# A Mamba block with a SwiGLU layer on one core: 32 products per batch, whose results nobody reads, are left out

## The reference

```
h  = x * rsqrt(mean(x*x) + 1e-5) * norm_w
xs, res = split(h @ in_proj_w.T)                      # 256 + 256 channels
u  = silu(causal conv of 4 taps over xs + conv_b)
delta, Bm, Cm = split(u @ x_proj_w.T)                 # 64 + 16 + 16
delta = softplus(delta @ dt_proj_w.T + dt_proj_b)
state[t] = exp(delta[t] * A) * state[t-1] + delta[t]*u[t]*Bm[t]   # 256 channels x 16 states
y  = (sum over states of state*Cm + u*D) * silu(res)
x1 = layernorm(x + (y @ out_proj_w.T + x))
out = layernorm(x1 + (silu(x1 @ wg.T) * (x1 @ wu.T)) @ wd.T)      # 384 hidden
```

## Time and profile before

| | us |
|---|---|
| median of 3 runs | 560.69 (560.64 to 561.02) |
| the profiled execution, its own time | 562.91 |
| its span, first to last instruction | 561.1 |
| PE busy | 522.8 |
| DVE busy | 495.8 |
| POOL busy | 414.2 |
| ACT busy | 385.8 |

### The profile page before, as it was taken

The page is one execution under the profiler, slowest core; times in us unless marked ns, Lnnn a source line. Parts: engine busy times, 40 slices in busy tenths (PEclk is TensorE's granted clock), DMA queues, the critical chain, the costliest instruction groups (busy, mean ns, idle before and its releaser), DMA issues.

```text
span 561.1 us, 7049 instructions
## 1 busy us (share of the span) xinstructions
PE 522.8 (93%) x2161; PEld 272.9 (49%) x2161; DVE 495.8 (88%) x559; ACT 385.8 (69%) x625; POOL 414.2 (74%) x212
## 2 busy tenths in 40 slices
PE   8989998999999999999999999999999997668695
PEld 6444444545564536545564536544564534433363
DVE  5867789998999999999999999999999999998863
ACT  3676896599478975699478974799478974554231
POOL 8769677996579874996589874996589874996310
PEclk9979999999999999999999999999999999759798
DMA  8062305600624032700624032600634042700000
GB/s 224 9 151 56 96 8 143 151 0 2 150 59 111 1 73 78 167 4 0 151 62 108 0 82 70 169 0 0 150 63 106 0 90 60 168 2 0 0 20 19
DMA packets 27391, 39.29 MB, mean 70 GB/s; under 512 B 3832, under 2 KB 10072, under 8 KB 27360
## 3 DMA queue, kind: packets, MB, share of 16 engines
q1 hardware_dynamic: 25168, 38.38, 28.7%
q10 hardware_dynamic: 2192, 0.55, 0.5%
HBM read 3.27 MB, written 2.10 MB: 10 GB/s over the span
## 4 chain that ended last, share of the span: by engine, by line
PE 74%; DVE 9%; issue 6%; ACT 5%; POOL 2%; DMA 1%; SPq 1%; POOLq 0%; DVEq 0%; ACTq 0%
PE dense_ps L508 18%; PE y_ps L500 9%; PE dense_ps L526 9%; PE dense_ps L577 7%; DVE state L1196 6%; PE dense_ps L584 3%; PE c_ps L484 3%; PE dense_ps L528 2%; PE dense_ps L533 2%; PE dense_ps L545 2%; PE y_ps L498 2%; PE dense_ps L547 2%; PE dense_ps L551 2%; PE dense_ps L549 2%; PE dense_ps L541 2%
## 5 line engine op out<-in xcount | busy, mean ns | idle before, releaser
L1018 POOL TENSOR_TENSOR prod<-du_rep,b_rep 128x2048 f32<-128x2048 f32 x63 | 286.0, 4544 | 71.9 <-ACT b_rep L778 50.0
L1196 DVE TENSOR_TENSOR_SCAN state<-decay_ps,prod 128x512 f32<-128x512 f32 x256 | 298.9, 1207 | 17.3 <-ACT decay_ps L731 10.6
L731 ACT ACTIVATE decay_ps<-delta_rep,a_neg 128x512 f32<-128x512 f32 x252 | 170.0, 689 | 71.8 <-DVE state L1196 71.6
L1206 DVE TENSOR_TENSOR state<-state,c_ps 128x1536 f32<-128x1536 f32 (+1 forms) x63 | 122.8, 1949 | 19.0 <-PE c_ps L484 14.8
L508 PE MATMUL dense_ps<-x_all,ident 128*128 128x256 f32 x476 | 121.8, 398 | 5.6 <-ACT z_pos L757 3.6
L508 PEld LDWEIGHTS dense_ps<-x_all,ident 128*128 128x128 f32 x476 | 88.5, 195 | 48.4 <-issue 15.6
L500 PE MATMUL y_ps<-state,gather 128*32 128x512 f32 x504 | 70.8, 635 | 4.6 <-DVE state L1206 4.6
L526 PE MATMUL dense_ps<-h_t,tap_t 128*128 128x512 f32 x128 | 58.4, 598 | 0.9 <-ACT h_t L789 0.9
L1040 POOL TENSOR_TENSOR state<-state,c_rep 128x512 f32<-128x512 f32 x40 | 51.4, 1285 | 4.3 <-ACT c_rep L774 4.2
L484 PE MATMUL c_ps<-bc,pick 64*128 64x512 f32 x64 | 31.6, 493 | 8.4 <-DVE state L1206 8.4
L526 PEld LDWEIGHTS dense_ps<-h_t,tap_t 128*128 128x128 f32 x128 | 23.2, 189 | 30.5 <-issue 29.4
(11 more groups left out here) (201 smaller groups left out, 691.3 us busy)
## 6 DMA issues: line engine op xcount, KB each, us to landing
du_rep<-z_wm SPq DMA_DIRECT2D x64, 256.0 KB, 5.0
delta_rep<-z_ln SPq DMA_DIRECT2D x64, 256.0 KB, 4.5
out_dram<-y_out SPq DMA_DIRECT2D x7, 256.0 KB, 4.7
state<-L_attn_in_proj_w_in ACTq DMA_DIRECT2D x1, 256.0 KB, 3.9
x_all<-L_attn_x_in SPq DMA_DIRECT2D x1, 256.0 KB, 4.2
state<-L_ffn_w_gate_in SPq DMA_DIRECT2D x1, 192.0 KB, 10.0
state<-L_ffn_w_up_in SPq DMA_DIRECT2D x1, 192.0 KB, 3.5
state<-L_ffn_w_down_in SPq DMA_DIRECT2D x1, 192.0 KB, 4.3
```

The lines of the kernel that those rows point to most:

```text
L731: A(decay_ps[n % DECAYS][:, :], decay_ps[n % DECAYS][:, :] if spread_first else delta_rep[:, h, c, :], ACT.Exp, scale=a_neg[:, col:col + 1 ...
L1018: TT(prod[quad % 2][:, :, :], du_rep[:, h, :, :], b, ALU.mult).then_inc(prod_ready, 1)
L1196: dve.tensor_tensor_scan(state[n // BLOCKS % 2][:, n % BLOCKS, :], decay_ps[n % DECAYS][:, :], prod[n // BLOCKS % 2][:, n % BLOCKS, :], 0. ...
L1206: TT(state[quad % 2][:, mine, :], state[quad % 2][:, mine, :], c_ps[:, :].unsqueeze(1).broadcast_to([P, BLOCKS - mine.start, T]), ALU.mult ...
```

## The change

All 32 "F" entries are taken out of `PLAN`. The real jobs keep their order. `stir` itself, the idle products of head and tail, all tables of the other engines and all waits of the real jobs stay as they were.

```diff
-        PLAN = [["Fh", "Fh", "Fh", "Fh", "Fh", "Fh", "Fh", "Fh", "C", "Fh", "S", "h"],
+        PLAN = [["C", "S", "h"],
                 ["proj", "xs0", "C", "S", "xs1"],
-                ["res0", "res1", "C", "Fxd", "Fxd", "Fxd", "Fxd", "Fxd", "S"],
-                ["xd", "Fz0", "Fz0", "S", "x1", "Fz0", "Fz0", "z0", "C"],
-                ["z1", "Fgate0", "Fgate0", "Fgate0", "Fgate0", "Fgate0", "S", "Fgate0", "Fgate1", "Fgate1", "Fgate0", "Fgate0", "Fgate1", "gate0", "C", "gate1", "d0"],
+                ["res0", "res1", "C", "S"],
+                ["xd", "S", "x1", "z0", "C"],
+                ["z1", "S", "gate0", "C", "gate1", "d0"],
                 ["S", "gate2", "C", "d1", "b0"],
-                ["up0", "up1", "up2", "S", "Fb1", "b1", "C", "down", "Fb2", "Fb2"],
+                ["up0", "up1", "up2", "S", "b1", "C", "down"],
                 ["b2", "b3", "C", "S"]]
```

## The result

The changed kernel takes 572.17 us (median of 4 runs, 571.72 to 572.79). The kernel before, run beside it, takes 560.86 us. The ratio is 1.0206, with a 95% interval of 1.0188 to 1.0224: slower by 11.3 us. The profiled execution of the changed kernel took 571.72 us and spans 569.7 us, 8.6 us more than the span of before. The rest of the 11.3 us is that the profiled execution of before lay 2.2 us above its median and this one does not.

The account below looks back on a forecast made before the run. DVE was taken as nearly full (58.75 of 62.93 us a batch), with PE setting the end in two gap-free stretches. Per batch 2.7 + 1.0 + 1.5 - 2.1 = +3.1 us, seven times +21.7: median 582 us, range 549 to 606.

Parts of the forecast that it names:

- the likeliest case: The forecast itself: the clock falls at the start and in the middle of each batch; 570 to 604 us, chance 0.54.
- Idle time and fall of the clock at the start: Ahead of C of quad 0: PE idles 4.6 us in every batch, and the clock is expected to fall each time.
- First cost: Start of a batch, C to `proj` partly at half rate: 2.7 us lost one for one, range 1.7 to 3.3.
- Second cost: Light middle: waits let the clock fall, `z0` and `z1` slow down, ACT waits; 1.0 us, range 0 to 1.5.
- Third cost: Second stretch, from `z_ln` on: if the clock is low then, gap-free work runs late; 1.5 us, range 0 to 3.3.
- The gain: Idle products on the path removed, at full clock: 2.1 us won per batch, between 0.6 and 4.2.
- the 0.6 us of the product behind C: Between C of quad 0 and S: two idle passes delay the whole first stretch; removing them wins 0.6 us.
- The 1.1 us of the middle: Ahead of `gate0`: idle products make C of quad 4 late; about 1.1 us of DVE's 1.8 us wait is won.
- The 0.4 us behind `b1` and `down`: Idle products ahead of `b1` and behind `down` delay POOL's input for the next batch; removing them wins 0.4 us.
- Seven times the same: Seven preparing batches each grow by 3.1 us, +21.7 us in all; the last batch changes by 0.
- Faster by small losses: Rival: the low clock hardly touches real work, so removed waits win; 549 us, from 543 to 558, chance 0.17.
- A clock that stays low for much of the batch: Rival: half rate makes PE bound the batch; +7 to +10 us a batch, 610 to 632 us, chance 0.12.

Follow-up runs that it names:

- e5: Against the kernel before, only the eight idle products of `h` ahead of C of quad 0 kept, the other 24 left out: 553.04 us, ratio 0.9857.
- e7: Against e5, each idle product of `h` and the head's three use 32 rows of the array, not 128: 574.49 us, ratio 1.0220.
- e1: Against the changed kernel, the nine idle products of `h` at the start of a batch put back: 553.0 us, ratio 0.9857.
- e8: Against e5, twelve idle products of `h` ahead of C of quad 0, not eight: 559.13 us, ratio 0.9970.
- e9: Against e5, the eight idle products written into the bank of `proj`, not of `h`: 553.62 us, ratio 0.9867.
- e6: Against e5, four idle products of `h` ahead of C of quad 0, not eight: 555.54 us, ratio 0.9892.
- e4: Against e3, the six idle products between S of quad 3 and `gate0` left out too: 553.79 us, ratio 0.9890.
- e3: Against the kernel before, four idle products left out: one between C of quad 0 and S, one of `b1`, two of `b2`: 556.65 us, ratio 0.9927.
- e10: Against e4, the eight idle products of `h` left out, the 14 of the middle kept: 564.16 us, ratio 1.0071.
- e2: Against the kernel before, idle products of `h`, `b1` and `b2` left out, the 20 of the middle kept: 567.11 us, ratio 1.0113.

## Why the prediction was right, and where it was off

The direction and the range held, and the likeliest case was the one that came: the clock falls at the start of each batch and again in the middle. The size was off: 582 us forecast, 572.2 measured. Against e5, where neither cost shows, a steady batch of the changed kernel is 64.8 - 61.5 = 3.3 us longer, and e5's is 63.0 - 61.5 = 1.4 us shorter than that of before. So the costs are 3.3 us where 5.2 were forecast, and the gain is 1.4 us where 2.1 were: errors on both sides, which in part cancel. By its steps:

**Idle time and fall of the clock at the start.** Right. The wait was 4.36 us (4.6 forecast), and the clock went to half just ahead of C, for 6.7 us. e7 shows the cause, e1 and e5 that filling this place alone removes it.

**First cost, 2.7 us.** Right for PE. The stretch from C to the end of `res1` grew by 18.93 - 16.80 = 2.13 us, although it lost the 0.63 us of the idle product: 2.76 us. "One for one" was wrong: DVE's wait at scan 11 grew from 0.30 to 2.50, so 2.2 us reached the batch. The rest went into the slack that e8 shows.

**Second cost, 1.0 us for `z0` and `z1`.** This step failed. They ran at full rate (1.45 us for the last three passes), ACT did not wait for them, and the clock fell only behind them, at S of quad 3. The cost was 0.

**Third cost, 1.5 us.** Right in kind, a little large. The product on `z_ln` was 1.34 us behind `z_ln`, and 0.31 us before (263.19 against 262.88 in the timeline of before): 1.0 us. DVE's wait of 1.44 us for C of quad 5 is what it turned into; it is 0.25 us in e5, so the cost is 1.2 us a batch. In e5 the clock fell in the middle too, in three of the five batches in two short pieces and in two in one of 6.8 us, and it was at full rate again when `z_ln` came; the windows of one of the three:

```profile
303.40:306.70 3.30, 2.84 (x12) 0.92 (x12) 3.30 (x4) 3.28 (x6) 3.30 (x1) 0.50 0.00 0
...
310.20:313.50 3.30, 2.92 (x10) 0.71 (x10) 3.30 (x4) 3.30 (x7) 3.30 (x2) 0.50 0.00 0
313.60:320.00 6.40, 4.98 (x12) 1.87 (x11) 6.37 (x7) 6.35 (x8) 4.92 (x2) 1.00 0.00 0
```

`z_ln` is ready at 318.49 + 1.06 = 319.55 us there. Whether the clock is low until `z_ln` comes is what the prediction said the cost depends on, and the traces bear it out: the low stretch ends 40.5 us after the mark in the changed kernel, and 38.4 to 38.5 us after it in the batch of e9 above, in two of e8 and in one of e6, and DVE waits 1.1 to 1.5 us there. Where it ends 36.1 us after the mark or earlier, as in all steady batches of e1 and e5, the wait is 0.25 us. With the start at half rate and the middle not filled this came in every steady batch (changed kernel, e7), with the start filled only now and then. A slow start is not needed for it, as e9 shows; why it comes each time behind one stays open.

**The gain, 2.1 us.** Too large: 1.4 us, by e1 and e5 against before. Of its items, the 0.6 us of the product behind C is nothing (e5 against e1, 61.5 and 61.6 us). The 1.1 us of the middle is 0.5 (e4 against e3), as DVE then waits for ACT. The 0.4 us behind `b1` and `down` is rather 0.8 (e3 against before, if the product behind C counts for nothing). The prediction took ACT's wait of 0.15 us for `res1` as proof that PE has no slack; e5 and e8 show a ring over one bank and a slack of about 0.7 us.

**Seven times the same.** This failed. A steady batch grew by 1.84 us and not 3.1, and the iterations around them did not follow. The first two scanned batches together grew by 1.0 us (first mark 161.8 against 160.8). In k = 0 of before, the nine idle products took 5.7 us, partly at half rate, ahead of `h`; that they are gone may have given back what the clock took, which was not tried by itself. From the last mark to the end it is 83.9 us, and it was 85.5: the wait for C of quad 4 in the last batch, 1.8 us in the timeline of before, is gone. The profile's sum is 1.0 + 5 x 1.84 - 1.6 = 8.6 us, which is 569.7 - 561.1.

**The rivals.** Faster by small losses: e1 shows that a gain is real, but it is 1.4 us a batch, and the 2.2 us of the first cost that reached DVE exceed it alone. The figure of the Trainium skill that stood beside it ("TensorE: Matmul & The Clock Gate", Part 1: ramping costs under 1% of a typical kernel's span) is given there for the cold matmuls at a kernel's start. It does not carry over to a clock that falls again in every batch: changed kernel against e5 is 19.1 us, 3.5%. A clock that stays low for much of the batch: it was low for 16.8 of 64.8 us.

## What to carry to other kernels

Products that nobody reads can pay where PE's real work has a wait ahead of a stretch that everyone else waits for: here 8 of 32 gave all of the benefit, and the other 24 cost 1.4% (553.0 against 560.9 us). Those of the middle paid only while the start was not filled (e10). Fill the place that comes just before the critical stretch, size it to the wait (four were 2.5 us worse by the median, though within the spread of the runs, and twelve 6 us worse than eight), and use all rows of the array. Price a cost where the bounding engine feels it: PE lost 2.76 us at the start of a batch, DVE 2.2. A short wait of one engine for another is no proof that the other has no slack: look whether it in turn waits for the first one's bank.

## What the runs showed of the hardware

At the start of a batch the granted clock followed not how long PE was occupied but how many rows of the array its products used. Sixteen passes of 3.9 us in all over 32 rows let the clock fall to half (0.50), in all five steady batches of e7, where sixteen passes of 3.7 us over 128 rows held it at 1.00 in all five of e5, in the same place of the same kernel. Other numbers of rows, and fewer columns, were not tried. The Trainium skill ("TensorE: Matmul & The Clock Gate", Part 1) says that the gate is set by how busy PE has been recently. If that is read as PE's busy time in the profile, 3.90 of 3.90 us in e7, the trace disagrees. At half rate S took 1.93 us and not 1.07, and the first part of `proj` 1.92 to 2.08 and not 1.06.

A program whose work repeats can also settle into a rhythm with the clock. In the changed kernel each of the last four steady batches lasted 64.8 to 64.9 us with the clock falling at the same point; in e2 and e10, where PE has the same wait of 4.4 us ahead of C, the batches last from 62.5 to 64.6 us, and the fall comes at another moment in each. In e10 it came once 2.9 us ahead of C (222.2 against 225.10), so that a part of its 6.8 us was spent idle, and DVE waited 1.42 us at scan 11; 0.7 us ahead of C the wait was 2.46 us. That is the way in which the prediction worked out its first cost.
